# Images loaded one slot further ahead of their shift copies, with 32 slots unrolled

## The reference

```python
patches = img.reshape(Bn, C, N_P, P, N_P, P)
patches = patches.transpose(0, 2, 4, 1, 3, 5).reshape(Bn, N_P * N_P, IN_DIM)
tokens = jnp.einsum('bsd,hd->bsh', patches, W) + b
h = concatenate([cls, tokens], axis=1) + pos
h = h + attn(layernorm(h))     # causal linear attention, decay 0.9, width 128
h = h + ffn(layernorm(h))      # 8-head softmax attention
```

## Time and profile before

| | |
|---|---|
| median of 3 runs | 989.46 us (986.82 to 997.56) |
| profiled execution | 983.08 us, span 981.0 us |
| TensorE busy | 866.9 us (88%), 8112 matmuls |
| VectorE busy | 611.6 us (62%) |
| ScalarE busy | 539.5 us (55%) |
| GpSimd busy | 321.2 us (33%) |
| queue 1 of the DMAs (SyncE's and ScalarE's) | 147.86 MB, 61.4% of 16 engines |
| mean granted TensorE clock | 0.933 |

### The profile page before, as it was taken

How to read it: one execution, slowest core, us unless ns; L and a number is a source line. 1 busy time by engine, 2 the same in 40 slices (tenths; PEclk the granted TensorE clock), 3 DMA queues, 4 the chain that set the end, 5 groups by cost and what they waited for, 6 DMA issues and landing times.

```text
span 981.0 us, 27005 instructions
## 1 busy us (share of the span) xinstructions
PE 866.9 (88%) x8112; PEld 764.2 (78%) x8112; DVE 611.6 (62%) x1956; ACT 539.5 (55%) x1300; POOL 321.2 (33%) x848
## 2 busy tenths in 40 slices
PE   1477779999999989799899998999989999999997
PEld 1466678888888878689789787879878888888785
DVE  2135566757676676467666667567756676677673
ACT  0234345566466655456556655556566466556565
POOL 1565433323333332223332434233333333332100
PEclk9979899979899999789998999799989898999899
DMA  6555677666766765665766676676667666754550
GB/s 170 154 152 151 142 180 174 167 155 167 166 166 162 170 172 150 160 157 151 167 169 161 153 178 167 152 166 171 166 153 171 168 160 152 184 120 85 107 119 19
DMA packets 128241, 150.98 MB, mean 154 GB/s; under 512 B 11838, under 2 KB 122574, under 8 KB 122702
## 3 DMA queue, kind: packets, MB, share of 16 engines
q1 hardware_dynamic: 124432, 147.86, 61.4%
q10 hardware_dynamic: 3646, 1.19, 0.7%
HBM read 30.99 MB, written 6.46 MB: 38 GB/s over the span
## 4 chain that ended last, share of the span: by engine, by line
PE 37%; SPq 23%; DMA 19%; issue 8%; DVE 4%; POOL 4%; ACTq 2%; ACT 1%; POOLq 1%; DVEq 0%
SPq L232 11%; DMA img<-in_x 10%; PE ps L420 6%; DMA img<-img 6%; PE ps L536 5%; PE ps L577 5%; SPq L253 5%; PE ps L560 5%; SPq L222 3%; DMA stack<-qk 2%; SPq L239 2%; PE ps L609 2%; PE ps L466 2%; SPq L244 2%; PE ps L509 2%
## 5 line engine op out<-in xcount | busy, mean ns | idle before, releaser
L786 DVE TENSOR_REDUCE top<-ps 99x2 f32<-99x394 f32 x512 | 268.7, 560 | 153.2 <-PE ps L536 151.1
L918 ACT ACTIVATE prob<-ps 99x396 f32<-99x396 f32 x512 | 229.2, 499 | 48.9 <-PE ps L560 47.1
L536 PE MATMUL ps<-stack 66*99 66x198 f32 x1024 | 207.2, 287 | 14.1 <-DMA stack<-qk 9.0
L560 PE MATMUL ps<-stack 68*99 68x198 f32 x1024 | 188.6, 268 | 33.6 <-ACT prob L918 33.2
L873 ACT ACTIVATE cols<-img 126x588 f32<-126x588 f32 (+1 forms) x128 | 135.0, 1057 | 128.7 <-DMA img<-img 118.9
L420 PE MATMUL ps<-w_tok,cols 126*99 126x128 f32 x1280 | 175.4, 290 | 12.4 <-ACT cols L873 12.4
L536 PEld LDWEIGHTS ps<-stack 66*99 66x99 f32 x1024 | 140.1, 174 | 57.9 <-issue 41.1
L560 PEld LDWEIGHTS ps<-stack 68*99 68x99 f32 x1024 | 138.5, 173 | 41.5 <-ACT prob L918 39.7
L420 PEld LDWEIGHTS ps<-w_tok,cols 126*99 126x99 f32 x1280 | 160.1, 181 | 12.6 <-issue 12.6
L577 PE MATMUL ps<-prob,v_ones 99*32 99x198 f32 (+1 forms) x2048 | 114.9, 342 | 0.4 <-ACT prob L918 0.4
L345 POOL TENSOR_TENSOR var<-mv,eps 99x2 f32<-99x2 f32 x64 | 12.7, 198 | 241.7 <-DVE mv L729 241.6
(11 more groups left out here) (142 smaller groups left out, 1475.9 us busy)
## 6 DMA issues: line engine op xcount, KB each, us to landing
stack<-qk SPq DMA_DIRECT2D x256, 198.0 KB, 5.2
img<-in_x SPq DMA_DIRECT2D x192, 150.1 KB
img<-img SPq DMA_DIRECT2D x64, 449.4 KB
img<-img SPq DMA_DIRECT2D x64, 448.5 KB
out<-h SPq DMA_DIRECT2D x64, 49.5 KB
out<-h SPq DMA_DIRECT2D x64, 49.0 KB
stack<-top_rows SPq DMA_DIRECT2D x64, 12.4 KB
w_rows<-in_L_tok_W SPq DMA_DIRECT2D x1, 294.0 KB, 3.1
```

Source lines behind the costliest of these rows:

```text
L536: last = nc.tensor.matmul(ps[0:T, M0 + c % 2, j * SP:(j + 1) * SP], stack[b.ring % 4][0:BIAS_ROW, h, 0, qt * T:(qt + 1) * T], stack[b.ring ...
L560: last = nc.tensor.matmul(ps[0:T, E0 + c % 2, j * SP:(j + 1) * SP], stack[b.ring % 4][:, h, 1, kt * T:(kt + 1) * T], stack[b.ring % 4][:, ...
L786: nc.vector.tensor_reduce(top[:, c // 4, 2 * (c % 4):2 * (c % 4) + 2], columns, AX.X, ALU.max, negate=True).then_inc(m_read, 1)
L918: nc.scalar.activation(prob[:, c, :], ps[0:T, E0 + c % 2, 0:CHUNK], ACT.Exp, scale=DK ** -0.5).then_inc(exp_done, 1)
```

## The change

The lag of the shift goes from 1 to 2, and each later lag rises by one too. The plans themselves keep their order. The number of slots unrolled ahead of the loop (PEEL) is 32 and no longer 16, so that the loop turns twice and not three times. Where a plan asked by the slot's number whether a batch of four is due, it now asks by the image's, which picks the same images.

```diff
@@ -31,6 +31,7 @@
 RING = 16
+PEEL = 32
 BATCH = 4
@@ -71,9 +72,9 @@
-    for n in range(RING):
+    for n in range(PEEL):
         slot(Image(n // RING, n % RING))
-    with engine.Fori(1, B // RING) as turn:
+    with engine.Fori(PEEL // RING, B // RING) as turn:
         for u in range(RING):
             slot(Image(turn, u))
     for n in range(B, B + lag):
@@ -92,8 +93,8 @@
-SHIFTED, PATCHED, TURNED, ADDED, ROUTED = 1, 2, 3, 4, 8
-PROJECTED, STACKED, MAXED, TOPPED, MIXING, ENDING, STORED = 9, 10, 11, 12, 13, 14, 15
+SHIFTED, PATCHED, TURNED, ADDED, ROUTED = 2, 3, 4, 5, 9
+PROJECTED, STACKED, MAXED, TOPPED, MIXING, ENDING, STORED = 10, 11, 12, 13, 14, 15, 16
 IMGS, TURNS = 4, 8
@@ -565,7 +566,7 @@
-                    if b.ring % BATCH == (RING - MIXING) % BATCH and routed.exists():
+                    if routed.ring % BATCH == 0 and routed.exists():
@@ -614,7 +615,7 @@
-                routing = n.back(ROUTED) if n.ring % BATCH == 0 else Image(-1, 0)
+                routing = n.back(ROUTED) if n.back(ROUTED).ring % BATCH == 0 else Image(-1, 0)
@@ -818,8 +819,8 @@
-                choosing = n.back(ROUTED + 1) if n.ring % BATCH == 1 else Image(-1, 0)
+                choosing = n.back(ROUTED + 1) if n.back(ROUTED + 1).ring % BATCH == 0 else Image(-1, 0)
```

## The result

The changed kernel takes 896.93 us in the median of six runs (889.62 to 903.89), against 989.24 before: 0.9045 of it, with a 95% interval of 0.8994 to 0.9096. Forecast were 923 us in a range of 892 to 955, and faster. Its profiled execution has a span of 887.9 us, where that of before had 981.0. So 93 us went, half as much again as the 64 I had summed. The time lies inside the range, but also in the band of the second rival (870 to 905, chance 0.15) and outside that of the forecast proper (905 to 938).

What follows compares the result with a forecast made beforehand. SyncE's DMA queue was taken as the bound, with TensorE's 11.85 us a slot as floor; 53 slots at 12.9 plus one jump gave 688 against 752, gain 64, so 925, with the fill 923 us, range 892 to 955.

Steps and rivals of the forecast that it cites:

- the second rival: TensorE's clock stays full once the L560 stalls go: 12.3 us a slot, gain 97, 892 us; chance 0.15.
- the forecast proper: The main expected outcome, 923 us, in a band of 905 to 938; chance 0.62.
- The closed turn: SyncE's queue: each shift waits 2.9 us for the load just issued, in a 14.19 us slot; without it 11.3.
- Is the shift early enough?: SyncE's shift to ScalarE's column copy: 6.9 + 0.7 = 7.6 us to land against 7.8 available, 1.6 slack behind.
- The first rival: The shift collides with the load in the DMA queue and stays late: 13.4 us a slot, 953 us; chance 0.16.
- The routing term: TensorE's extra per four slots over 4 x 11.85: 1.6 + 0.3 us stalls and 2.3 low clock, 12.9 a slot.
- My sign for the fourth slot: In the trace, three slots of four were to take 11.9 us and the fourth 14 to 17.
- The clock before: TensorE's granted clock averaged 0.93 in the kernel before, 52 us lost, with low clock following idle stretches.
- The jump: The loop jumps back once, not twice: one TensorE issue wait of 2.0 us remains, plus 2.3 for its clock.
- my other bound: Unrolling slots 16 to 31 was to cost nothing extra; the bound on the other side was 2 us per 16.
- Nothing for the added slot: One more pipeline slot at the front, holding a load alone: between 0 and some 6 us, taken as 0.
- The third rival: Stack copies queued behind load and shift land late and TensorE waits: 1042 us with 1 us more; chance 0.03.

Runs made afterwards that it cites:

- the fully unrolled one: The changed kernel with all 64 slots as straight code and no loop; 891.66 us, ratio 0.9037 to the kernel before.
- the two doses: The changed kernel with four or ten further GpSimd copies right ahead of spread2 in the routing slots; 919.43 us with four, 991.58 us with ten.
- the added DMA: The changed kernel with one more 319 KB DMA a slot behind each shift pair, which ScalarE's column copy also waits for; 1016.34 us, ratio 1.0251.

## Why the prediction was right, and which terms were off

**The closed turn** was right, and opening it brought all but a few us of the gain. The wait for in_x went, SyncE waits for the low halves instead, and moving the load alone did the same. The unrolling alone left everything at 14.19. One reading in it was off: the two images 11.87 us apart do not show a loop boundary that let SyncE catch up. They come behind a slot of 17.2 us, and in the kernel with only the unrolling two slots of 11.8 come behind one of 18.3 with no boundary near. So a long slot of TensorE is enough to let the queue catch up.

**Is the shift early enough?** It was, but not by my sum. I had 7.6 us of landing against 7.8 of time. The time was 8.9 in a usual slot: shift issued at 447.96, column copy at 456.83. The difference is the stack's issue, which takes 2.61 us where I carried over 3.90. Before, it was issued 0.2 us behind the shift's; now 2.1 us lie between. The landing that I had at 6.9 + 0.7 took 7.6 to 11.8 us in the five slots that show it, three of them in the fill, against 6.4 to 8.4 before. So the collision with the load, which I cost at nothing, is there, and it cost little because the time had grown by 1.1 us more than I reckoned. The first rival's price did not come: five short waits for the shift in 53 slots, 3.6 us together. Its own sum is off as well: 53 slots of 13.375 us are 709 and not 712, which makes it 950 and not 953.

The ring-order rule of the Trainium skill (DMA: Bandwidth & Descriptors, Queues, rings and completion order) would have the shift complete behind the load. The trace agrees in direction, by the landings of up to 11.8 us; whether it is this order or the load on the DMA engines that delays the shift, no run here parts.

**The routing term** failed, and it is the term that put the forecast high: 688 us for the stretch, against 660.8. For four slots I had 1.6 + 0.3 us of stall and 2.3 of low clock over 4 x 11.85. The stalls were 1.0 (7.9 + 1.0 + 4.4 us over 13 batches), the clock nothing, and 1.0 was not in my sum at all: the routing's own matmuls, which the 11.85 of a usual slot doesn't hold. Over 13 batches that is 30 us less for the clock, 11 less for the stalls and 13 more for the matmuls. The slot of image 9, still in the fill at 9.1 us, takes off 3 more and the jump's slot puts on 4. Together that is the 27.

Without the jump's slot, which is 8.7 over its neighbours, the slots are (660.8 - 8.7) / 53 = 12.3, the number of the second rival (the clock holds), to which I gave 0.15. Its condition is what happened. That its number fits to the digit is luck: it holds 1.9 us of stall where 1.0 of stall and 1.0 of matmuls belong. My sign for the fourth slot, 14 to 17 us, did not show either: two slots of four took more than 11.9, one 13.1 and one 12.3 to 13.5.

I took 1.6 from two of the three long stalls of the kernel before (1.5 to 1.8); its others behind a choice were 0.6 at most, and the changed kernel's 0.2 to 1.3, 0.7 in the mean. And I took the clock from three slots, two of which were followed by half rate, as if their own stalls of 1.5 to 1.8 us had been the cause each time. In the changed kernel none of 13 routing slots was followed by it, in the fully unrolled one 1 of 13, and with stalls put in of the size I had priced, 3 of 9. So at the stalls that came, the clock behind them should have stood in the sum at next to nothing.

**The clock before** then needs its cause in the sum. It took 52 us, nearly as much as the idling of 57. With SyncE's wait gone, both went together. Behind image 10 the kernel before had a low clock in 16 slots. In 13 of them it fell right after TensorE had waited 1.1 to 3.0 us for the exponential (L560), the wait that the closed turn caused (six of these had 0.3 to 0.6 us behind a choice as well); in two it fell behind a choice alone and in one at a jump. So most of the clock's loss went by the cause that the change took away, and I had priced it where it mostly wasn't. I counted the idling as the effect of the turn and the clock as its follower, which the two doses bear out: 31 us of stalls in lumps of 3 cost 68 in clock. That 9 us in lumps of 1.4 cost 14 shows that the price isn't in proportion to the idle time.

**The jump** I had at 2.0 + 2.3. The slot took 20.5 where its neighbours in the pattern took 11.8, 8.7 more: 4.9 us of waiting for instructions, the rest at half clock. One jump was saved and the other waited longer than the two had (4.0 us). The nine kernels here with 32 unrolled slots waited 3.4 to 7.2 us in all at their one jump, the three with 16 waited 4.0, 4.3 and 5.8 at their two. So the unrolling saved no waiting of this kind, and my other bound, a further 2 us per 16 slots, was the nearer one; why it is so, no run shows. In the time of several runs the jump is small or lost in the scatter, as the unrolled kernel shows.

**Nothing for the added slot** was right: the first 112 us are 0.6 shorter. The "few us in the fill" that took 925 to 923 I had for images 10 to 12, which are inside the stretch already. The wait of load for the buffers, which I put at nothing in the steady slots, is nothing there.

**The third rival** I excluded by counting how busy the DMA engines were: 0.67 before, 0.77 now. It didn't happen (TensorE's waits for stack copies are 1.5 us), but the reason was weaker than I wrote. I had reckoned that the transfers would have to slow each other by a quarter; with a seventh more bytes they did so by more, as these three show. The busy time of a slot is 0.77 x 12.47 = 9.6 us in the changed kernel, 0.67 x 14.19 = 9.5 before, and 0.94 x 14.84 = 13.9 with the added DMA: 4.3 us more for 319 KB, where 450 KB of loads and 900 KB of shifts and all the rest take 9.6. Whether it is the engines that all these copies share, or the partitions that the shifts and the added copy both read, wasn't tried and stays open.

## What to carry to other kernels

When one engine's queue issues all DMAs in a fixed order, add up its turn: if a wait for a landing stands first and the transfer it waits for was issued last, the landing is part of the turn, and moving one step in the list is worth as much as a deeper pipeline. Price the stalls of TensorE by their lumps and not by their sum: here 0.7 us every fourth slot cost about itself, and 31 us of stalls in lumps of 3 cost 89 in all, the clock with it. And look for the work that only some slots have before you multiply a usual slot: here it was 1.0 us every fourth. And don't take 0.77 busy DMA engines for a quarter of free bandwidth before a run with more bytes has shown it.

## What the runs showed of the hardware that I had not expected

- A DMA of 319 KB per slot that nothing waits for, 14% more bytes, made the kernel 15% slower by the ratios (1.0441 over 0.9045), and what moved per second fell from 186 to 179 GB/s in the run with the same DMA waited for.
- Shifts issued right behind the next image's load (0.04 to 0.14 us) landed 7.6 to 11.8 us after their issue in the five slots that show it; in the kernel before, which waited for its load first, they took 6.4 to 8.4.
- The issue of the same four stack DMAs took SyncE 3.90 us directly behind the shift's issue and 2.61 us when 2 us lay between.
- 1.0 us of GpSimd copies behind the write of the choice cost nothing: the gap of 1.45 us that stood there, at a register load, shrank to 0.32; the same copies ahead of spread2 cost 2.5% (0.9267 over 0.9045).
- After stalls of nearly the same size (1.4 to 1.8 us) the granted clock fell to 1.2 GHz in three slots of nine and stayed at 2.4 GHz in the others; after the same pair of 0.46 and 0.82 us it fell in one kernel and not in another. The profile doesn't show what parts them.
